# Score-bound norms moved ahead of the last attention product, and weight binarization moved from GpSimd and ScalarE to VectorE, in a transformer layer on eight cores

## The reference

```python
def attn(x, W_Q, W_K, W_V, W_O, b_Q, b_K, b_V, b_O):
    q = einsum('bpd,hde->bphe', x, W_Q) + b_Q      # k and v alike
    scores = einsum('bqhe,bkhe->bhqk', q, k) / sqrt(128)
    scores = where(tril, scores, -100000.0)
    z = einsum('bkhe,bhqk->bqhe', v, softmax(scores))
    return einsum('bqhe,hed->bqd', z, W_O) + b_O

def ffn(x, weight, bias):
    alpha = mean(abs(weight), axis=1, keepdims=True)
    bw = where(weight >= 0, 1.0, -1.0) * alpha
    return einsum('bsi,oi->bso', x, bw) + bias

x = x + layernorm(attn(layernorm(x), ...))
x = x + layernorm(ffn(layernorm(x), weight, bias))
```

## Time and profile before

| | |
|---|---|
| device time, median of 2 runs | 2754.2 us (2752.51 to 2755.89) |
| the profiled execution's own time | 2752.0 us |
| its span, slowest core (core 1) | 2750.5 us |
| spans of the eight cores | 2742.4 to 2750.5 us |
| mean granted TensorE clock, all cores | 0.846 to 0.850 of full speed |

### The profile page before, as it was taken

The page is one execution under the profiler, slowest core; times in us unless marked ns, Lnnn a source line. Parts: engine busy times, 40 slices in busy tenths (PEclk is TensorE's granted clock), DMA queues, the critical chain, the costliest instruction groups (busy, mean ns, idle before and its releaser), DMA issues.

```text
span 2750.5 us, 27156 instructions; the slowest of 8 cores (2742.4 to 2750.5 us)
## 1 busy us (share of the span) xinstructions
PE 1924.4 (70%) x8336; PEld 824.8 (30%) x8336; DVE 951.7 (35%) x1712; ACT 588.1 (21%) x769; POOL 326.2 (12%) x574
## 2 busy tenths in 40 slices
PE   2568678687786786786877877861317778778774
PEld 1323233232232332332332322321213333333332
DVE  3532332333223223323322333232223453353353
ACT  1213303213113123033032131231111111111110
POOL 1001101101011011011011111114440000000000
PEclk9679889898898898898998988975658889889887
DMA  6321122121121120221212413203220221221210
GB/s 147 114 31 24 14 25 24 12 27 16 20 27 14 20 28 8 25 24 14 25 24 42 58 14 50 37 21 109 77 91 25 77 77 41 75 77 50 66 54 31
DMA packets 178473, 119.31 MB, mean 43 GB/s; under 512 B 168100, under 2 KB 168100, under 8 KB 170148
## 3 DMA queue, kind: packets, MB, share of 16 engines
q0 software_dynamic: 107200, 75.51, 16.1%
q1 hardware_dynamic: 71140, 42.07, 5.7%
HBM read 125.97 MB, written 25.17 MB: 55 GB/s over the span
## 4 chain that ended last, share of the span: by engine, by line
PE 50%; DVE 16%; ACT 10%; issue 8%; POOL 6%; DMA 5%; DVEq 4%; ACTq 1%; POOLq 0%; SPq 0%
PE psA L358 8%; PE psB L358 8%; PE psE L636 7%; ACT ptil L568 5%; PE psC L823 5%; PE psC L358 4%; DMA c<-fw 3%; DVEq L58 3%; POOL c L419 3%; PE psC L600 3%; DVE st L210 3%; PE psD L823 2%; PE psE L823 2%; POOL ptil L590 2%; PE psD L358 2%
## 5 line engine op out<-in xcount | busy, mean ns | idle before, releaser
L619 DVE TENSOR_TENSOR ptil<-ptil,c 128x512 bf16<-128x512 bf16 x640 | 220.4, 421 | 505.1 <-ACT c L609 490.0
L358 PE MATMUL psA<-arena_a,wbuf 128*128 128x512 bf16 x1024 | 305.5, 385 | 4.9 <-ACT arena_a L276 3.1
L358 PE MATMUL psB<-arena_a,wbuf 128*128 128x512 bf16 x1024 | 303.9, 384 | 2.8 <-ACT arena_a L276 2.8
L590 POOL TENSOR_TENSOR ptil<-ptil,tri_sb 128x128 bf16<-128x128 bf16 x256 | 108.6, 424 | 1010.4 <-ACT ptil L568 1010.3
L636 PE MATMUL psE<-ptil,v 128*128 128x512 bf16 x640 | 189.3, 390 | 51.7 <-DVE ptil L619 51.7
L568 ACT ACTIVATE ptil<-psA,mbias 128x1024 bf16<-128x1024 f32 x160 | 178.6, 1116 | 204.9 <-PE psA L554 124.8
L600 PE MATMUL psC<-ptil,onem_sb 128*128 128x512 bf16 x640 | 184.9, 404 | 50.5 <-POOL ptil L587 24.0
L823 PE MATMUL psC<-arena_a,c 128*128 128x512 bf16 x512 | 167.7, 412 | 57.4 <-DVE c L810 57.4
L504 ACT ACTIVATE srow<-srow 1x1 f32<-1x1 f32 x16 | 3.3, 203 | 820.3 <-DVE srow L500 820.3
L568 ACT ACTIVATE ptil<-psB,mbias 128x1024 bf16<-128x1024 f32 x160 | 177.4, 1109 | 0.4 <-PE psB L554 0.2
L554 PE MATMUL psA<-qt,kt 128*128 128x512 bf16 x320 | 110.7, 431 | 77.4 <-ACT ptil L568 50.2
(11 more groups left out here) (121 smaller groups left out, 2377.4 us busy)
## 6 DMA issues: line engine op xcount, KB each, us to landing
c<-fw POOLq DMA_DIRECT2D x16, 1024.0 KB, 5.3
ptil<-x SPq DMA_DIRECT2D x16, 1024.0 KB, 6.4
out<-wbuf POOLq DMA_DIRECT2D x16, 1024.0 KB, 4.6
wbuf<-wq POOLq DMA_DIRECT2D x16, 512.0 KB, 8.2
wbuf<-wk POOLq DMA_DIRECT2D x16, 512.0 KB, 8.3
c<-x SPq DMA_DIRECT2D x8, 1024.0 KB, 5.0
wbuf<-wv POOLq DMA_DIRECT2D x16, 512.0 KB, 8.3
zs<-c SPq DMA_DIRECT2D x64, 128.0 KB, 2.0
```

The costliest lines, as they stand in the source:

```text
L358: e.matmul(banks[bidx], wslot[sl][:, c * 128:(c + 1) * 128], ln1t3[:, c, s * SLW:(s + 1) * SLW], start=(c == 0), stop=(c == NCH - 1)),
L590: gp_mask_j[j] = p.op("gpsimd", lambda e, j=j, r=r: e.tensor_tensor(ptil[:, j * GQ + r * 128:j * GQ + (r + 1) * 128], ptil[:, j * GQ + r * ...
L619: dv_norm[j] = p.op("vector", lambda e, j=j, g=g: e.tensor_tensor(pslot[j], pslot[j], rbc[g % 2], ALU.mult), wait=wait, inc="DV")
```

## The change

Four things are moved.

1. The Q half of the bound (square, four matmuls, maxima, logarithm) is emitted for head h+1 right behind Q's matmuls at the end of head h, so ahead of the product L636. Head 0 has it where it was.
2. The square of K is emitted behind K's copies and ahead of V's. Its four matmuls stand behind V's matmuls and wait for V's copies (same banks).
3. The small matmul for `mbias` and its copy are emitted behind the first two score matmuls.
4. In stage 3 the comparison and the two copies of the transposed halves go to VectorE, and GpSimd's list keeps the loads alone.

```diff
@@ emit_bw_tile
-        p.drain("gpsimd")
-        gp_ge = p.op("gpsimd", lambda e, fpar=fpar: e.tensor_scalar(
-            fwst[fpar], fwst[fpar], 0.0, None, ALU.is_ge),
-            wait=[("DV", dv_as)], inc="GP")
+        p.drain("vector")
+        p.op("vector", lambda e, fpar=fpar: e.tensor_scalar(
+            fwst[fpar], fwst[fpar], 0.0, None, ALU.is_ge))
         p.drain("vector")
         dv_bw = p.op("vector", lambda e, fpar=fpar: e.tensor_scalar(
             v_sb[:], fwst[fpar], twoal[:, 0:1], negal[:, 0:1],
-            ALU.mult, ALU.add),
-            wait=[("GP", gp_ge), ("PE", pe_bw_last)], inc="DV",
+            ALU.mult, ALU.add), inc="DV",
...
-            p.drain("scalar")
-            sc_bw_evac_half[half] = p.op(
-                "scalar", lambda e, t=t, b=b, c0=c0, c1=c1: e.copy(
+            dv_bw_evac_half[half] = p.op(
+                "vector", lambda e, t=t, b=b, c0=c0, c1=c1: e.tensor_copy(
                     bwt3[:, c0:c1, t * 128:(t + 1) * 128],
@@ new functions, the old code of the head loop in four pieces
+    def emit_mh_sq(which, h):
+        src = (qt_sb, kt_sb)[which]
+        if which == 0:
+            w0 = [("DV", dv_qkv_evac_d[(h, 0)]), ("PE", pe_mb_prev),
+                  ("PE", pe_bw_last), ("PE", pe_norm_last)]
+        else:
+            w0 = [("DV", dv_qkv_evac_d[(h, 1)]), ("PE", pe_norm_last)]
+        dv_sq_d[which] = p.op("vector", lambda e, s=src: e.tensor_mul(
+            sqb, s[:], s[:]), wait=w0, inc="DV")
+
+    def emit_mh_mms(which, h):
+        for s in range(NSL):
+            hb = s % 4
+            wait = [("DV", dv_sq_d[which]), ("CONST", const_t),
+                    ("SC", psbuf_last_rd[hb])]
+            if which == 1:
+                wait.append(("DV", dv_red_d[(0, s)]))
+            if s == 0 and (which == 1 or h == 0):
+                wait.append(("DV", dv_qkv_evac_d[(h, 2)]))
...
@@ head loop
         if h > 0:
             emit_w_mms(h, 1)
+            emit_mh_sq(1, h)
             emit_w_mms(h, 2)
...
+        if h == 0:
+            emit_mh_sq(0, 0)
+            emit_mh_mms(0, 0)
+            emit_mh_sq(1, 0)
+        emit_mh_mms(1, h)
+        emit_mh_tail(h)
...
             if (j + 1) % estep == 0:
+                if not mb_done:
+                    emit_mb(h)
+                    mb_done = True
                 emit_exp(0, j + 1 - estep, pe_sc, sc_exp)
...
             elif h + 1 < H:
                 emit_w_mms(h + 1, 0)
+                emit_mh_sq(0, h + 1)
+                emit_mh_mms(0, h + 1)
```

More of the change, by code:

```diff
@@ L433, in emit_bw_tile @@
             c1 = NCH if half else hn2
-            wait = [("DV", dv_bw), ("SC", sc_bw_evac_half[half]),
+            wait = [("DV", dv_bw), ("DV", dv_bw_evac_half[half]),
                     ("DV", dv_zevac.get(gidx - 1, 0))]
@@ new lines, in emit_mh_mms @@
+    def emit_mh_mms(which, h):
+        nonlocal pe_norm_last, dv_red_last, sc_lns
+        for s in range(NSL):
[6 more added lines that the diff above has]
+                wait.append(("DV", dv_qkv_evac_d[(h, 2)]))
+            pe_norm_last = p.op("tensor", lambda e, s=s, hb=hb: e.matmul(
+                [psA[:, 0:SLW], psA[:, 512:512 + SLW], psB[:, 0:SLW],
+                 psB[:, 512:512 + SLW]][hb], onem_sb[:],
+                sqb[:, s * SLW:(s + 1) * SLW], start=True, stop=True),
+                wait=wait, inc="PE")
+            dv_red_d[(which, s)] = p.op(
+                "vector", lambda e, s=s, hb=hb, wh=which: e.reduce_max(
+                    srow[0:1, wh * 8 + s:wh * 8 + s + 1],
+                    [psA[0:1, 0:SLW], psA[0:1, 512:512 + SLW],
+                     psB[0:1, 0:SLW], psB[0:1, 512:512 + SLW]][hb], AX.X),
+                wait=[("PE", pe_norm_last)], inc="DV")
+        p.drain("vector")
+        dv_mx_d[which] = p.op("vector", lambda e, wh=which: e.reduce_max(
+            srow[0:1, 16 + wh:17 + wh], srow[0:1, wh * 8:wh * 8 + NSL],
+            AX.X), inc="DV")
+        dv_red_last = dv_mx_d[which]
+        p.drain("scalar")
+        t_ln = p.op("scalar", lambda e, wh=which: e.activation(
+            srow[0:1, 18 + wh:19 + wh], srow[0:1, 16 + wh:17 + wh], AF.Ln,
+            bias=0.0, scale=1.0), wait=[("DV", dv_mx_d[which])],
+            inc="SC" if which == 1 else None)
+        if which == 1:
+            sc_lns = t_ln
@@ new lines, in emit_mh_tail @@
+    def emit_mh_tail(h):
+        nonlocal dv_nm_cur
+        p.drain("vector")
+        dv_add = p.op("vector", lambda e: e.tensor_tensor(
+            srow[0:1, 20:21], srow[0:1, 18:19], srow[0:1, 19:20], ALU.add),
+            wait=[("SC", sc_lns)], inc="DV")
+        sc_M = p.op("scalar", lambda e: e.activation(
+            srow[0:1, 21:22], srow[0:1, 20:21], AF.Exp,
+            bias=lncb_sb[0:1, 0:1], scale=0.5),
+            wait=[("DV", dv_add)], inc="SC")
+        p.drain("vector")
+        dv_nm_cur = p.op("vector", lambda e: e.tensor_scalar(
+            nm_bf[:], srow[0:1, 21:22], -1.0, None, ALU.mult),
+            wait=[("SC", sc_M)], inc="DV", lowp="softmax shift operand; "
+            "softmax is shift-invariant so the value need not be exact")
@@ new lines, in emit_mb @@
+    def emit_mb(h):
+        nonlocal pe_mb_prev, dv_mbias, dv_mbias_prev
+        pe_mb = p.op("tensor", lambda e: e.matmul(
+            psC[:, 0:1], oner_sb[:], nm_bf[:], start=True, stop=True),
+            wait=[("DV", dv_nm_cur), ("DV", dv_qkv_evac_d[(h, 1)]),
+                  ("SC", sc_rinv_prev)], inc="PE")
+        pe_mb_prev = pe_mb
+        dv_mbias = p.op("vector", lambda e: e.tensor_copy(
+            mbias[:], psC[:, 0:1]), wait=[("PE", pe_mb)], inc="DV")
+        dv_mbias_prev = dv_mbias
@@ L469, in build_program @@
                     inc="WO", incn=16)
[L471 to L523, removed]
```

33 lines of the change are left out of this document (15 added, 18 removed).

## The result

The changed kernel takes 2671.3 us (median of 11 runs), the kernel before, beside it, 2752.3 us (median of 10). The ratio is 0.9697, 95% interval 0.9677 to 0.9717: 81 us less. The profiled execution took 2669.8 us; its slowest core is core 4.

A forecast was written before the change was run, and what follows sets the result against it. Bounds: TensorE's waits inside heads, and stage 3's unoverlapped chain of 13.0 us a tile. Gains of 73 (stage 3) + 2 (heads) = 75 us from 2752.0 gave 2677, with 2 between profiled and median 2679, stated as 2678; range 2645 to 2712.

The forecast's parts named there:

- Heads, 2 us gained: All heads together: 112 us gained after V plus 1 in head 0, less 111 paid after Q.
- V's end: V's last matmul to the first score matmul: 10.5 us instead of 18.3, 7.7 less; net 7.5 a head.
- Q's end: Matmuls on Q's squares wait ahead of the product: 4.6 idle + 1.7 + 1.1 = 7.4 us lost a head.
- The clock's part: After the idling, the four norm matmuls and 5.3 product matmuls run slow; without clock loss 5.5 us a head, not 7.4.
- Stage 3, 73 us gained: Weight tiles: pitch 8.6 us instead of 13.0; 65 us saved from first to last sum, 8 at the end.
- The late load: Stage 3, where stage 4's first loads come at the same time: 2 us of the earlier 8 left.
- The projection after tile 4: Stage 3: it holds TensorE 15.8 us, so tile 5's transposes wait; 8 us more.
- A: Rival: clock not lost after Q or back sooner, perhaps kept up after V; 2650, down to 2640; chance 0.17.
- B: Rival: the whole product runs slow, 33 us lost in the heads against 73 gained; 2712; chance 0.09.
- C: Rival: loads or a 2.3 us comparison set stage 3's pitch; 2693 for one us more, 2709 for two; chance 0.10.
- D: Rival: slower than before, as the clock does not come back before K's projection; 2916; chance 0.03.
- E: Rival: V's transposes can't start as psA is held, only 3 to 4 of 7.5 us gained; 2734; chance 0.04.

The follow-up runs named there:

- e1: Changed kernel with stage 3's tile code of the kernel before (parts 1 to 3 alone): 2748.0 us against 2751.1, ratio 0.9990.
- e3: Changed kernel with the matmuls on Q's squares behind the product instead of ahead of it: 2576.2 us, ratio 0.9364 to the kernel before.
- e4: Changed kernel with 20 unread matmuls filling TensorE's wait ahead of the matmuls on Q's squares: 2649.7 us, ratio 0.9631 to the kernel before.
- e2: Kernel before with only the new stage 3 tile code (part 4 alone): 2676.2 us against 2751.1, ratio 0.9728.
- e10: Kernel before without GpSimd's drain ahead of each comparison, loads where they were: 2752.4 us against 2751.0, ratio 1.0004.
- e5: Kernel before with tile t+2's load issued right behind tile t's comparison in GpSimd's list; expected about 2692 us, measured 2743.3 against 2751.1.
- e8: Kernel before with loads issued ahead, right behind the comparison, and GpSimd's drain before each comparison removed: 2692.0 us against 2753.8, ratio 0.9777.

## Why the prediction was right, point by point

The forecast was 2678 us and 75 us gained; measured were 2671.3 and 81. It rests on two sums, and each can be held against a run.

**Heads, 2 us gained.** e1 gives 3.1, with an interval that includes nothing. The trace gives 1.1 us in head 0 (1.2 forecast) and 0.1 in each of the 15 others. That it is a balance, and not an absence of effects, e3 shows: with most of the payment taken away, 95 us appear.

Both sides of the balance were a little too small, by about the same. V's end: 7.7 forecast, 8.3 measured as the mean distance. The two gaps ahead of TensorE's next work, taken as 0.37 and 0.36, are 0.15 each (617.46 to 617.61, 621.01 to 621.16). `mbias` gives back 0.3, not 0.2. Q's end: 7.4 forecast, 7.9 measured. That the net came out so close is in part luck: each side alone was short by some 8 us over the 15 heads, and these errors cancel.

The parts of Q's end, on the mean: idle 4.67 (4.59 taken from V's end of the kernel before), the four matmuls 1.66 (1.7), the product 1.4 longer (1.1). The last 0.16 is an overlap that is lost: in the kernel before, the product starts that much before the modelled end of Q's last matmul. The clock's part was forecast as 0.8 for the four matmuls and 1.1 for the product, 1.9; e4 measures 1.8, as 0.4 and 1.4. So its sum was right and its division was not. At the fast level the four are 0.34 apart and not 0.22, and in the product some 6 matmuls are slow on the mean, 2 to 10 from head to head, where one place in the trace before had given 5.3.

The rule of the Trainium skill weighed there, "TensorE: Matmul & The Clock Gate", section "HAM oscillation — how this bites in real kernels", is borne out at Q's end: filling the wait with work, and nothing else, brought 22 us.

**Stage 3, 73 us gained.** e2 gives 75. From first to last sum the trace has 134.1 us (1855.95 to 1990.04), forecast 139, before 204.5. The pitch is 8.25 instead of 8.6. A third of that is the comparison, 1.23 us instead of L865's 1.35, which had also been taken as the lower end; the rest is latency that I had rounded up. The late load costs 0.4 us, not 2. The projection after tile 4 costs 9.6 (17.9 from one sum to the next), not 8. The end, 7.8 us against 7.6, is as forecast.

**The rivals.** A (the clock stays up): out at Q's end, where the four matmuls start 0.38 to 0.43 us apart in all 15 heads. At V's end it happened for a moment. Behind the wait of 2.98 us all four matmuls took 376 ns in 4 of the 15 heads, which made V's end at most 0.2 us shorter, and the group of queries behind is no faster than before (11.43 against 11.15 on the mean). B (the whole product slow): out, it took 4.1 to 5.75 us, and 16 matmuls 0.43 apart would take 7.0. C: the loads were in time, but for 0.26 us at one tile. D: K's projection ran at the high level. E: the transposes started at once.

**What the prediction did not see.** Its reading of stage 3, "of which no part overlaps another", is true of the kernel before, and the drain adds nothing to that chain (e10). The forecast did not need the drain, since the change empties GpSimd's list of both the comparison and the drain. The expectation for e5 did, and missed by 51 us.

## What to carry to other kernels

When code is moved off a chain's end by putting it into another list, the new place has neighbours: here the matmuls on Q's squares stood ahead of 16 matmuls that had been ready, and a change worth 8 us a head gave 0. Put the early work behind what is ready and ahead of what waits anyway; two lines of order were worth 95 us. And before an engine gets the blame for a slow stage, undo its order alone: the comparison on GpSimd cost 5.35 us a tile, but 61 us, against the 75 of stage 3's part of the change, could be had without moving it.

## What the runs showed of the hardware

A drain on GpSimd's list waits for a load that GpSimd has itself issued, until it lands. With the drain between the two (e5), the comparison started 0.25 or 0.26 us after the load's landing in 14 of 16 tiles, with loads that took 4.9 to 10.6 us, and the profile put 75.4 us of idle time before 14 of the 16 comparisons down to no semaphore. Without it (e8) the comparison started 1.8 us after the issue in 13 tiles, 3.3 to 10.5 us ahead of the landing. In the profile this idle time reads "issue", which is easily taken for the cost of issuing. What ended the idle time before e5's comparisons (us in all, times):

```profile
  issue: 75.4, 14
```

against, in e8_ahead_no_drain, the same question:

```profile
  DVE asum L421: 35.5, 16
```

The comparison with one constant takes 1.23 us on VectorE in f32, 128x2048, in place; the multiplication and addition with two scales read from memory (L426) take 1.35 on the same shape, with a bf16 result, and L865, which also reads two such scales, takes 1.35 with an f32 one. Which property makes the 0.12 us was not tried.
